# Best-32 cross attention on one Trainium2 core: a shorter exact search, and a count in place of a fifth search

## The reference, cut to what matters

```python
Q = (x_text @ Wq).reshape(B, T, 4, 32)          # B=2, T=256, 4 heads
K = (x_vision @ Wk).reshape(B, G, 4, 32)        # G=4096 keys
scores = einsum('bthd,bghd->bhtg', Q, K) / sqrt(32)
topv, topi = top_k(scores, 32)                  # the 32 best keys of each row
probs = softmax(topv, axis=-1)
attn = zeros_like(scores).at[..., topi].set(probs)
c_t = einsum('btg,bgd->btd', attn.mean(axis=1), x_vision @ Wv)
```

## Time and profile before

| | us |
|---|---|
| median of 3 runs | 1135.57 |
| lowest, highest run | 1134.72, 1139.25 |
| the profiled execution | 1138.91 |
| its span in the trace | 1137.6 |
| PE, PEld busy | 951.6 (84%), 591.3 (52%) |
| VectorE (DVE) busy | 840.6 (74%) |
| ScalarE (ACT) busy | 649.2 (57%) |
| GpSimd (POOL) busy | 297.8 (26%) |
| mean granted TensorE clock, share of full speed | 0.893 |

### The profile page before, as it was taken

One profiled execution on the slowest core, in us unless ns is written; L12 is line 12 of the kernel. 1 busy time (PEld: TensorE's weight loads), 2 busy tenths in 40 slices (PEclk: granted clock), 3 DMA queues, 4 the chain that ended last, 5 costly groups with the idle time before them and its releaser, 6 DMA issues. The chain is left out here.

```text
span 1137.6 us, 20939 instructions
## 1 busy us (share of the span) xinstructions
PE 951.6 (84%) x7724; PEld 591.3 (52%) x7724; DVE 840.6 (74%) x1742; ACT 649.2 (57%) x1048; POOL 297.8 (26%) x314
## 2 busy tenths in 40 slices
PE   5997859999999999997889989157888888987585
PEld 5976724444444444443548875133555556634353
DVE  4775678999999989951457976998888884266447
ACT  3442306788878878885345425069999997202111
POOL 1000088899600000000023521006473631000010
PEclk9999957999999999998799996567799988997798
DMA  5867651322223222200412228002362236830000
GB/s 177 308 236 275 236 138 50 82 77 75 78 76 83 78 78 74 77 13 3 112 43 84 71 70 212 1 1 61 110 171 84 65 98 203 193 119 1 0 1 19
DMA packets 99321, 111.84 MB, mean 98 GB/s; under 512 B 26658, under 2 KB 75730, under 8 KB 99218
## 3 DMA queue, kind: packets, MB, share of 16 engines
q1 hardware_dynamic: 96802, 109.50, 32.7%
q10 hardware_dynamic: 2416, 0.99, 0.4%
HBM read 80.95 MB, written 29.43 MB: 97 GB/s over the span
## 5 line engine op out<-in xcount | busy, mean ns | idle before, releaser
L835 ACT ACTIVATE pT<-bank 128x512 f32<-128x512 f32 x512 | 278.4, 597 | 96.7 <-PE bank L752 75.8
L857 DVE TENSOR_REDUCE rmax<-bank 128x2 f32<-128x1024 f32 x256 | 307.3, 1222 | 29.7 <-PE bank L720 28.8
L764 PE MATMUL bank<-pT,V 128*17 128x256 f32 x2048 | 162.3, 389 | 4.7 <-ACT oT L841 4.6
L1736 PE MATMUL bank<-K1s,qs 97*128 97x512 f32 x256 | 117.4, 561 | 54.4 <-ACT below L1845 36.6
L752 PEld LDWEIGHTS bank<-qs,ks 49*128 49x128 f32 x1024 | 78.3, 188 | 113.5 <-ACT pT L835 100.0
L2000 POOL TENSOR_TENSOR total<-total,work 128x1024 f32<-128x1024 f32 x40 | 94.8, 2379 | 159.5 <-ACT work L1854 158.6
L752 PE MATMUL bank<-qs,ks 49*128 49x256 f32 x1024 | 130.8, 334 | 2.3 <-ACT pT L835 0.5
L720 PE MATMUL bank<-ks,qs 49*128 49x512 f32 x512 | 111.3, 430 | 16.9 <-DMA ks<-k_parts_d 9.7
L1736 PEld LDWEIGHTS bank<-K1s,qs 97*128 97x128 f32 x256 | 55.0, 227 | 69.5 <-ACT below L1845 38.0
L1906 DVE MAX8 cand<-work 128x8 f32<-128x128 f32 x384 | 76.5, 279 | 0.0
L764 PEld LDWEIGHTS bank<-pT,V 128*17 128x17 f32 x2048 | 34.5, 95 | 63.8 <-ACT pT L835 42.0
(11 more groups left out here) (463 smaller groups left out, 1829.4 us busy)
## 6 DMA issues: line engine op xcount, KB each, us to landing
k_parts_d<-kparts SPq DMA_DIRECT2D x48, 512.0 KB
ks<-k_parts_d SPq DMA_DIRECT2D x381, 64.0 KB, 2.2
K1s<-k_parts_d SPq DMA_DIRECT2D x96, 128.0 KB
cn<-in_ctx SPq DMA_DIRECT2D x32, 384.0 KB, 3.6
cx<-in_ctx SPq DMA_DIRECT2D x16, 384.0 KB, 5.2
w<-in_L_ffn_w SPq DMA_DIRECT2D x32, 128.0 KB, 2.4
w2e<-in_L_ffn_w SPq DMA_DIRECT2D x16, 128.0 KB, 2.7
W<-in_L_xattn_W SPq DMA_DIRECT2D x2, 1024.0 KB, 7.4
```

The lines of the kernel that those rows point to most:

```text
L764: t = pe.matmul(bank[32 * c:32 * c + VW, 7, a * S:(a + 1) * S], V[:, b * NCH + 4 * g + c, h, :], pT[:, (at + 2 * (c // 2) + a) % 8, c % 2 ...
L835: p_made.up(act.activation(pT[:, at % 8, :], bank[:, 4 + at % 3, :], ACT.Exp))
L857: max_read.up(dve.tensor_reduce(rmax[p % 2][:, :, qt, c], bank[:, b0:b0 + 2, :], AX.X, ALU.max))
L1736: m = pe.matmul(bank[:, b0 + c, :], qs1[0:NROW1, b * H1 + h, q], K1s[h][0:NROW1, keys], start=True, stop=(what == "new"))
```

## The change

It does three things, all in the phase described above.

1. The test of the candidates. The fourth MATCH_REPLACE8 and the fifth MAX8 over 256 candidates go; a TENSOR_SCALAR with an accumulator counts in each row the candidates at or above the 32nd. `over` becomes (worst >= 32nd) + count, which is 32 in a settled row, and the branch compares the sum over the rows with 128 x 32 instead of 0.
2. The exact path. Its first MAX8 over 4096 columns goes (the 8 largest are taken from the candidates), and so does the pass of L1944 over 4096 columns. For such a tile ScalarE's mark is computed with scale 1 and bias 1e30 instead, which is zero where LOW stands and 1e30 elsewhere.
3. For that, the scale of L1845 becomes a column in SBUF, `steep`, instead of a constant. GpSimd sets it to -STEEP at the start, and again behind each tile's `below` for t < 14; `settle` waits for that (`steep_usual`) instead of for `below_made`.

```diff
--- before.py
+++ after.py
@@ -1585,16 +1585,16 @@
     GC = 128
     NG = S2 // GC
     NQ = 8
-    NEX = 10
+    NEX = 9
     NCN = 4
-    LOW = -3e38
+    LOW, FAR = -3e38, 1e30
     STEEP = 2.0 ** 66
     below = sb("below", [P, S2], BF16)
     minus = sb("minus", [P, P], BF16)
     cand = sb("cand", [P, NG, 8])
     cleft = sb("cleft", [P, NG * 8])
     top = [sb(f"top{j}", [P, KTOP]) for j in range(2)]
-    rest8 = sb("rest8", [P, 8])
+    count, steep = sb("count", [P, 1]), sb("steep", [P, 2])
     worst, over = sb("worst", [P, 1]), sb("over", [P, 1])
     over_i = [sb(f"over_i{j}", [1, 1], I32) for j in range(2)]
     ntop, steep_thr = sb("ntop", [P, 2]), sb("steep_thr", [P, 2])
@@ -1615,8 +1615,8 @@
     cn_in = [flag(f"cn_in{j}") for j in range(NCN)]
     s_made, s_taken, sel, over_made, over_summed, over_in, exact, picked = (flag(n) for n in (
         "s_made", "s_taken", "sel", "over_made", "over_summed", "over_in", "exact", "picked"))
-    lsum_made, ebias_made, added, below_made, e_summed = (flag(n) for n in (
-        "lsum_made", "ebias_made", "added", "below_made", "e_summed"))
+    lsum_made, ebias_made, added, below_made, steep_usual, e_summed = (flag(n) for n in (
+        "lsum_made", "ebias_made", "added", "below_made", "steep_usual", "e_summed"))
     late_added = flag("late_added")
     total_turned, aT_made, c0_made, c0_copied, tm_in, tmask_made, c0_turned, c0T_made = (flag(n) for n in (
         "total_turned", "aT_made", "c0_made", "c0_copied", "tm_in", "tmask_made", "c0_turned", "c0T_made"))
@@ -1843,7 +1843,7 @@
                 act.wait_ge(*s_made.at(nth["cut", t - 1, k + n - 1] + 1))
             part = slice(k * 1024, (k + n) * 1024)
             below_made.up(act.activation(below[:, part], home(t)[:, part], ACT.Relu, bias=steep_thr[:, t % 2:t % 2 + 1],
-                                         scale=-STEEP), n)
+                                         scale=steep[:, t % 2:t % 2 + 1]), n)
 
         def exps(t, k):
             at = nth["cut", t, k]
@@ -1917,13 +1917,17 @@
             if t >= 2:
                 dve.wait_ge(*ebias_made.at(t - 1))
             take8(top[j][:, 0:8], cand[:, :, :].rearrange("p g k -> p (g k)"), cleft[:, :], sel)
-            for k in range(1, KTOP // 8):
+            for k in range(1, KTOP // 8 - 1):
                 take8(top[j][:, 8 * k:8 * k + 8], cleft[:, :], cleft[:, :], sel)
+            dve.wait_ge(*sel.at(sel.n))
+            sel.up(dve.max(top[j][:, KTOP - 8:KTOP], cleft[:, :]))
             dve.tensor_reduce(worst[:, :], cand[:, :, 7], AX.X, ALU.max)
+
             dve.wait_ge(*sel.at(sel.n))
-            sel.up(dve.max(rest8[:, :], cleft[:, :]))
+            sel.up(dve.tensor_scalar(cleft[:, :], cand[:, :, :].rearrange("p g k -> p (g k)"), top[j][:, KTOP - 1:KTOP], None,
+                                     ALU.is_ge, ALU.add, accum_out=count[:, :]))
             dve.wait_ge(*sel.at(sel.n))
-            over_made.up(dve.tensor_scalar(over[:, :], worst[:, :], rest8[:, 0:1], top[j][:, KTOP - 1:KTOP], ALU.max, ALU.is_ge))
+            over_made.up(dve.tensor_scalar(over[:, :], worst[:, :], top[j][:, KTOP - 1:KTOP], count[:, :], ALU.is_ge, ALU.add))
 
         def over_to_sbuf(t):
             dve.wait_ge(*over_summed.at(t + 1))
@@ -1934,16 +1938,15 @@
         def settle(t):
             j = t % 2
             dve.wait_ge(*over_in.at(t + 1))
-            if t >= 2:
-                dve.wait_ge(*below_made.at(4 * (t - 1)))
+            dve.wait_ge(*steep_usual.at(max(t + 1, 2)))
             dve.reg_load(flagged, over_i[j][0:1, 0:1])
-            with dve.If_ne(flagged, 0):
-                for k in range(KTOP // 8):
+            with dve.If_ne(flagged, P * KTOP):
+                exact.up(dve.match_replace(home(t)[:, :], top[j][:, 0:8], home(t)[:, :], LOW))
+                for k in range(1, KTOP // 8):
                     take8(top[j][:, 8 * k:8 * k + 8], home(t)[:, :], home(t)[:, :], exact)
-                dve.wait_ge(*exact.at(NEX * t + 8))
-                exact.up(dve.tensor_scalar(home(t)[:, :], home(t)[:, :], LOW, -1e18, ALU.not_equal, ALU.mult))
-                exact.up(dve.memset(steep_thr[:, j:j + 1], 0.0))
-            with dve.If_eq(flagged, 0):
+                exact.up(dve.memset(steep[:, j:j + 1], 1.0))
+                exact.up(dve.memset(steep_thr[:, j:j + 1], FAR))
+            with dve.If_eq(flagged, P * KTOP):
                 dve.tensor_scalar(steep_thr[:, j:j + 1], top[j][:, KTOP - 1:KTOP], STEEP, None, ALU.mult).then_inc(exact.sem, NEX)
             dve.wait_ge(*exact.at(NEX * (t + 1)))
             picked.up(dve.tensor_scalar(ntop[:, j:j + 1], top[j][:, 0:1], -1.0, None, ALU.mult))
@@ -1988,7 +1991,12 @@
         copy_c0(NGRP - 1)
 
     def best_pool():
+        for j in range(2):
+            steep_usual.up(pool.memset(steep[:, j:j + 1], -STEEP))
         for t in range(LATE):
+
+            pool.wait_ge(*below_made.at(4 * (t + 1)))
+            steep_usual.up(pool.memset(steep[:, t % 2:t % 2 + 1], -STEEP))
             if t % H1 == 0:
                 continue
             acc = total[t // H1 % 3]
```

## The result

The changed kernel takes 1128.17 us (median of 19 runs, 1122.78 to 1133.96) where the kernel before takes 1135.53 (19 runs, 1127.46 to 1139.25): 7.4 us less by the medians. As a ratio it is 0.994 (95% interval 0.9923 to 0.9957), 6.8 us less (4.9 to 8.7). The forecast was 1132.0, with 1127.5 to 1136.8 as its range. A second timing beside other kernels, on another chip, gave 0.9959 (0.9935 to 0.9983), 4.7 us less (1.9 to 7.4).

What follows compares the result with a forecast made beforehand. It took one VectorE stall, then ScalarE in the steady pipeline, as the bounds (later TensorE and VectorE, in untouched code). Terms: -6.7 + 3.1 = -3.6 us, from the median 1135.57 to 1132.0 us; range 1127.5 to 1136.8.

Steps and rivals of the forecast that it cites:

- The exact path, -6.7 us: VectorE's stall on tile 0: first MAX8 and L1944 pass go, two small MEMSETs come; 6.7 us saved (6.5 to 6.8).
- The test of the candidates, 0: VectorE, each tile: the count saves about 0.43 us, 7 us in all, hidden by its wait for TensorE's sum; worth 0.
- The scale as a column, +3.1 us: ScalarE's L1845, 34 times: a column as scale adds 93 ns each, 3.2 us; 3.1 us (0 to 4.9) counted lost.
- so little is absorbed. I leave 0.1 for it: ScalarE's pauses for TensorE at L1854 were to take in only 0.1 us of the scale column's 3.2 us.
- GpSimd and the moved wait, 0: GpSimd's MEMSETs and `settle`'s wait for them cost 0, with 15 us to spare.
- no change: The outcome of a whole-kernel difference within about 0.5%, 5.7 us; chance 0.67.
- the rival of a free column: At ScalarE's L1845 the scale column costs nothing, so only the stall counts: -6.7 us, 1128.9 us; chance 0.22.
- VectorE's saving: Rival: VectorE paces the steady part, so its 7 us from the new test count too: -10.6 us, 1125.0; chance 0.04.
- ScalarE's waits for TensorE behind the stall: Rival: TensorE's clock returns later after the stall, these waits grow 3.2 us: 1135.2 us, no change; chance 0.09.
- one tile takes the exact path as before: Against the rival that the branch sends a second tile there, 31.7 us more stall: 1163.7 us; chance 0.05.

Runs made afterwards that it cites:

- skip alone: The kernel before with only the exact path's first MAX8 over 4096 columns removed: 0.9967 of before, 3.7 us less (1.2 to 6.1).
- three COPYs: The kernel before with three one-column COPYs, which nobody reads, behind each of ScalarE's 34 marks: 1.002 of before, 2.3 us more (0.1 less to 4.7 more).
- eight COPYs: The kernel before with eight one-column COPYs behind each of ScalarE's 34 marks: 1.0181 of before, 20.6 us more (16.7 to 24.5).

## Why the prediction was right or wrong

- **The exact path, -6.7 us: right.** 6.7 on the timeline from the branch's first instruction to `ntop`. The two MEMSETs overlap wholly and start 0.13 us ahead of `ntop`, less than the 0.2 taken. The kernel without the path (32.3 us in the time for 32.0 on the timeline) confirms that the stall counts in full, and skip alone agrees with it (3.7 for 4.5).
- **The test of the candidates, 0: right.** The count takes 483 ns and an accumulator read of its own behind it, within 0.41 to 0.82. VectorE saves 0.4 us a tile, and its wait for the sum grows by no less; with three times the amount and the other sign, 1.8 us showed.
- **The scale as a column, +3.1 us: the term that was mis-sized.** The duration was right: 2030 to 2040 ns became 2131 to 2133. The Trainium skill states about 93 ns for each pointer operand ("ScalarE: Activation LUTs", section "What ACT_TABLE_LOAD costs"), and the 91 to 103 ns of these traces agree for a scale on top of a bias. From start to start a mark takes 0.09 to 0.1 us more as well. What failed is the step from there to the time, "so little is absorbed. I leave 0.1 for it". Alone, the column cost 0.6 us (-1.5 to +2.6), and 8 us of extra work cost 2.3 (-0.1 to +4.7). Why is open. The forecast held the time of everything else fixed. In the runs TensorE's clock wasn't: with the column and with three COPYs it was higher and ScalarE's pauses were shorter, with eight COPYs it was lower and they weren't. The estimate at an equal clock gives the column 1.7 to 2.2 us, nearer to the forecast than the 0.6. That ScalarE's work was simply taken in by pauses isn't shown.
- **GpSimd and the moved wait, 0: right.** No wait of VectorE for GpSimd in any trace.
- **The sum.** With the measured term it is -6.7 + 0.6 = -6.1 us, 1129.4, within both intervals of the whole change (-4.9 to -8.7 and -1.9 to -7.4). The measured time is 3.8 us below the forecast, and the likeliest case was "no change", under 0.5%; the first timing gave 0.6% and the second 0.4%. The first lies outside the forecast's -3.6 and at the amount of the rival of a free column; the second holds both. That rival's reason is wrong in any case: the column isn't read for free. That the time fell inside the range owes something to its width, which was drawn to take in this rival.
- **The other rivals.** No gain from VectorE's saving shows; ScalarE's waits for TensorE behind the stall didn't grow (7.1 and 7.3 us); one tile takes the exact path as before.

What stays open is what moves TensorE's clock. As an estimate, it explains most of why eight COPYs cost so much more for their amount (20.6 of 22.1 us) than three (2.3 of 8.0). It was higher with more work on VectorE as well (0.900 against 0.894, four times the error). Whether the extra work itself shifts it, up in these kernels and down with eight COPYs, or something else in them does, no run here separates. For the whole change the same estimate can't be made: the stall lowers the mean clock by being there (0.911 in the runs without it, 0.898 with it, in one group), so a shorter stall raises it by itself. The distance between -6.1 and the -7.4 of the first medians is smaller than the error of either timing.

## What to carry to other kernels

An engine that is 95% busy in a steady stretch isn't yet a bound on which each nanosecond counts, and its idle 5% aren't a reserve that takes in whatever is added either: here 2.7, 8.0 and 22.1 us of extra work showed as 0.6, 2.3 and 20.6. Where the idle time is made of short waits for TensorE, give an added cost the whole range from a small part to its full amount, and set the granted clock of the runs beside their times before the difference is put down to the edit. A stall in which every other engine stands still is the opposite, worth its length: 32.0 us of it showed as 32.3. One pair of traces can differ by several microseconds in code that wasn't touched, so compare them stretch by stretch, and take the size of a small term from a kernel with that term alone.

## What the runs showed of the hardware

- A TENSOR_SCALAR with an accumulator appears as TENSOR_SCALAR_CACHE_REDUCE, 483 ns on 128x256 with one column operand, and a DVE_READ_ACCUMULATOR of about 0.09 us behind it; without an accumulator and with two columns a TENSOR_SCALAR on 128x256 takes 408 ns.
- A scale column on top of a bias column adds 91 to 103 ns to an ACTIVATE on 2048 columns, and 92 on the shortest of those on 1024 (1137 before, 1229 after). From the start of such an instruction on 2048 columns to the start of the next it adds 0.09 to 0.1 us, so the time is not hidden behind a neighbour.
- The same kernel's runs spread over 12 us (1127.46 to 1139.25), and much of that goes with the granted TensorE clock, which lay between 0.895 and 0.907 in the 19 runs of the changed kernel, some 7 us less time for each 0.01 more there, and 5 to 7 in the groups of the kernel before.
